# Attention heads in half legs: 256-query legs, a lead of 14 maxima, and score products issued in pairs of banks

## The reference

```python
x = L0_attn_x                                   # (2, 1024, 128)
h = _layernorm(x, axis=-1) * (1 + ca) + sa
q = (h @ Wq.T).reshape(N, S, 16, 8).transpose(0, 2, 1, 3)   # k and v likewise
energy = jnp.einsum('nhqd,nhkd->nhqk', q, k)
attn = jax.nn.softmax(energy / jnp.sqrt(jnp.float32(8)), axis=3)
out = jnp.einsum('nhql,nhld->nhqd', attn, v)
x = x + ga * out.transpose(0, 2, 1, 3).reshape(N, S, 128)
...
```

## Time and profile before

| what | value |
|---|---|
| median of 3 runs | 1158.91 us (1148.05 to 1160.96) |
| profiled execution, its own time | 1150.8 us |
| its span | 1149.3 us |
| PE busy | 1036.9 us, 90% |
| DVE busy | 968.1 us, 84% |
| ACT busy | 814.9 us, 71% |
| POOL busy | 520.9 us, 45% |
| attention with its score pass | about 61 to 381 us of the span |
| max products (L548) / scores (L667) / value products (L694) | 512 / 512 / 2048 instructions |
| reductions (L559) / exponentials (L675) | 256 / 512 |

### The profile page before, as it was taken

How to read it: one execution, slowest core, us unless ns; L and a number is a source line. 1 busy time by engine, 2 the same in 40 slices (tenths; PEclk the granted TensorE clock), 3 DMA queues, 4 the chain that set the end, 5 groups by cost and what they waited for, 6 DMA issues and landing times. The chain is left out here.

```text
span 1149.3 us, 21244 instructions
## 1 busy us (share of the span) xinstructions
PE 1036.9 (90%) x7771; PEld 648.5 (56%) x7771; DVE 968.1 (84%) x1309; ACT 814.9 (71%) x1621; POOL 520.9 (45%) x487
## 2 busy tenths in 40 slices
PE   6899999999999887889999999899999984699992
PEld 4222222222222334458998984468888964488992
DVE  6899999999995676979999996989999996767774
ACT  3279898999998644978888844888888922265561
POOL 5400431010101211027899991048999972256663
PEclk9779999999999988799999999899999995699996
DMA  5210100001000420107999980118999967311124
GB/s 158 69 43 15 30 16 21 25 16 30 15 2 2 130 56 2 58 2 178 244 248 224 223 205 3 58 43 193 234 242 224 242 144 253 41 43 41 43 48 121
DMA packets 58374, 114.40 MB, mean 100 GB/s; under 512 B 15406, under 2 KB 28718, under 8 KB 58272
## 3 DMA queue, kind: packets, MB, share of 16 engines
q0 software_dynamic: 14880, 50.23, 22.2%
q1 hardware_dynamic: 40152, 60.62, 16.8%
q10 hardware_dynamic: 3240, 2.20, 0.7%
HBM read 55.47 MB, written 9.13 MB: 56 GB/s over the span
## 5 line engine op out<-in xcount | busy, mean ns | idle before, releaser
L2245 PEld LDWEIGHTS m_pair<-filter_w,delta_x_t 128*128 128x128 f32 x2560 | 294.0, 192 | 43.1 <-issue 43.1
L559 DVE TENSOR_REDUCE neg_max<-max_ps 128x1 f32<-128x1024 f32 x256 | 295.6, 1214 | 15.2 <-PE max_ps L548 15.0
L2245 PE MATMUL m_pair<-filter_w,delta_x_t 128*128 128x112 f32 (+3 forms) x2560 | 298.5, 276 | 9.8 <-DVE h_t L2272 3.3
L675 ACT ACTIVATE exp_scores<-score_k 128x512 f32<-128x512 f32 x512 | 270.8, 605 | 28.4 <-PE score_k L667 22.7
L2221 ACT ACTIVATE decay<-delta,a_log 128x1024 f32<-128x1024 f32 x128 | 145.7, 1142 | 49.7 <-DVE normed L2272 29.7
L548 PE MATMUL max_ps<-k_rows,q_rows 48*128 48x512 bf16 x512 | 163.0, 400 | 12.4 <-DVE neg_max L559 10.7
L2213 ACT ACTIVATE filter_w<-filter,b_t 128x112 f32<-128x112 f32 (+1 forms) x576 | 167.4, 374 | 0.0
L667 PE MATMUL score_k<-q_rows,k_rows 51*128 51x512 bf16 x512 | 163.0, 389 | 2.4 <-ACT exp_scores L675 0.6
L694 PE MATMUL av_ps<-exp_scores,v_cols 128*32 128x256 f32 x2048 | 158.2, 394 | 0.0
L568 POOL CAST neg_max_parts<-neg_max 128x16 bf16<-128x16 f32 x16 | 3.2, 197 | 235.0 <-DVE neg_max L559 235.0
L694 PEld LDWEIGHTS av_ps<-exp_scores,v_cols 128*32 128x32 f32 x2048 | 44.2, 109 | 92.0 <-ACT exp_scores L675 52.8
(11 more groups left out here) (335 smaller groups left out, 1631.4 us busy)
## 6 DMA issues: line engine op xcount, KB each, us to landing
c_row<-c_rows SPq DMA_DIRECT2D x64, 512.0 KB, 6.0
x_inner<-normed POOLq DMA_DIRECT2D x16, 512.0 KB, 6.5
delta_x<-mod_memory POOLq DMA_DIRECT2D x15, 512.0 KB, 8.1
delta_x<-x_inner POOLq DMA_DIRECT2D x15, 512.0 KB, 8.3
x_inner<-h_t POOLq DMA_DIRECT2D x14, 512.0 KB, 5.7
mod_memory<-h_t POOLq DMA_DIRECT2D x14, 512.0 KB, 9.2
mod_memory<-normed POOLq DMA_DIRECT2D x12, 512.0 KB, 8.8
gate_up_all<-in_gate_up_w SPq DMA_DIRECT2D x8, 512.0 KB, 7.3
```

Of the source, the lines that this page charges most:

```text
L559: ve.tensor_reduce(nm[leg % 2][:, 4 * j + qt:4 * j + qt + 1], mps[:, bank:bank + 2, :].rearrange("p a q -> p (a q)"), AX_X, ALU.max, negat ...
L675: ac.activation(pt[a % 4][:, HEADS[r % 4], :], eps[:, bank, :], ACT.Exp, scale=SC).then_inc(*exped.up())
L2245: mm = pe.matmul(vps[blk][:, lo:hi], self.duT[b][:, c, blk * P:(blk + 1) * P], wf[g % 3][:, lo:hi], start=True, stop=True)
```

## The change

A leg of 512 queries is worked in two *turns* of 256 queries. Each turn has 8 max tiles, its own split, transpose, copy and 4 DMAs (half as many rows and queries in each), and 16 score banks. There are 32 turns in place of 16, issued at the end of places 0 and 2. The lead is 14 tiles instead of 22.

A score bank now holds two heads by 256 queries for one block of keys. Two banks are filled together by four products of 51 x 256 that alternate between the row halves (head 1, head 0, head 3, head 2), at the first s of each "msms"; the second s issues nothing. A pair waits for both of its banks. ACT still does 512 exponentials of 128 x 512, and `pe_av` is called as often as before. `po_ones(2, NS)` moves behind the split of turn 0, and the first `sp_load` of quad 1 waits for it.

```diff
-            nr = sb("neg_max_rest", [P, 4, 4])
-            ms = [sb(f"neg_max_parts{s}", [P, 4, 3, 4], BF16) for s in range(2)]
-            mt = [sb(f"neg_max_rows{s}", [48, P], BF16) for s in range(2)]
+            nr = sb("neg_max_rest", [P, 4, 2])
+            ms = [sb(f"neg_max_parts{s}", [P, 4, 3, 2], BF16) for s in range(2)]
+            mt = [sb(f"neg_max_rows{s}", [24, P], BF16) for s in range(2)]
...
-            NLEG, NU, AHEAD = BH // 2, 16, 22
+            NLEG, NU, AHEAD = BH // 2, 8, 14
+            NTURN, HQ = 2 * NLEG, CH // 2
...
-            def tile_of(leg, k):
-                return ((0, 2, 1, 3)[k // 4], k % 4) if leg == 0 else (k // 8 * 2 + k % 2, k % 8 // 2)
+            def tile_of(turn, k):
+                j, q = ((0, 2, 1, 3)[k // 2], k % 2) if turn == 0 else (k // 4 * 2 + k % 2, k % 4 // 2)
+                return j, turn % 2 * 2 + q
...
+            def sp_max_turn(turn):
+                leg, q0 = turn // 2, turn % 2 * HQ
+                sp.wait_ge(turn_read.sem, turn + 1)
                 for j in range(4):
                     s, row = head_rows(leg, j)
...
+                    sp.dma_start(qp[row + KR:row + KM, s, leg % 2, q0:q0 + HQ].rearrange("a (k q) -> a k q", k=2),
+                                 mt[turn % 2][6 * j:6 * j + 6, :]).then_inc(*max_in[turn % 2].up(16))
...
-            HEADS = (1, 3, 0, 2)
+            HEADS = ((1, 3), (0, 2))
+            def pe_score_pair(turn, r, banks):
+                leg, q0, kt = turn // 2, turn % 2 * HQ, r // 2
+                if r == 0:
+                    pe.wait_ge(max_in[turn % 2].sem, 64 * (turn // 2 + 1))
+                for _, free in banks:
+                    wait_from(pe, *free)
+                for c in range(2):
+                    for i, (bank, _) in enumerate(banks):
+                        s, row = head_rows(leg, HEADS[i][c])
+                        mm = pe.matmul(eps[:, bank, c * HQ:(c + 1) * HQ], kp[row:row + KM, s, kt * P:(kt + 1) * P],
+                                       qp[row:row + KM, s, leg % 2, q0:q0 + HQ], start=True, stop=True)
+                        if c:
+                            mm.then_inc(*score_mm.up())
...
             def score(e):
+                if e < 16 * NTURN and e % 2 == 0:
+                    banks = []
+                    for i in range(2):
+                        banks.append(score_bank())
+                        read.append((exped.sem, e + i + 1))
+                    pe_score_pair(e // 16, e % 16, banks)
+                    for i in range(2):
+                        ac_exp((e + i) // 16, (e + i) % 16, banks[i][0])
...
                     max_turn(0)
+                    po.wait_ge(*split.at())
+                    po_ones(2, NS)
+                    sp.wait_ge(*rows_set.at())
                     for half in range(2):
                         sp_load(1, half)
...
-                po.wait_ge(*part_lo.at())
-                po_ones(2, NS)
-                sp.wait_ge(*rows_set.at())
...
+                if place % 2 == 0 and n // 2 + 1 < NTURN:
+                    max_turn(n // 2 + 1)
                 if place == 2 and leg + 1 < NLEG:
-                    max_turn(leg + 1)
```

More of the change, by code:

```diff
@@ L544, in pe_max_score @@
                         pe.wait_ge(*first_half.at())
-                    elif k == (0 if leg else 8):
+                    elif k == (0 if turn else 4) and turn % 2 == 0:
                         pe.wait_ge(*loaded_at[leg // 2])
@@ L576, in max_score @@
             def max_score(v):
-                leg, k, half = v // 2 // NU, v // 2 % NU, v % 2
-                if leg >= NLEG:
+                turn, k, half = v // 2 // NU, v // 2 % NU, v % 2
+                if turn >= NTURN:
                     return
-                pe_max_score(leg, k, half)
+                pe_max_score(turn, k, half)
                 if half:
-                    ve_max_score(leg, k)
+                    ve_max_score(turn, k)
                     if k == NU - 1:
-                        po_max_parts(leg)
@@ L587, in pe_max_turn @@
-            def pe_max_turn(leg, bank, free):
-                pe.wait_ge(split.sem, 4 * leg + 4)
+                        po_max_parts(turn)
+            def pe_max_turn(turn, bank, free):
+                pe.wait_ge(split.sem, 4 * turn + 4)
                 wait_from(pe, *free)
                 pe.transpose(eps[:, bank, 0:64].bitcast(BF16)[0:3 * NU, :],
-                             ms[leg % 2][:].rearrange("p h a k -> p (h a k)"), self.identb[:]).then_inc(*max_turned.up())
-            def ac_max_turn(leg, bank):
-                ac.wait_ge(max_turned.sem, leg + 1)
-                wait_from(ac, max_in[leg % 2].sem, 64 * (leg // 2))
-                ac.activation(mt[leg % 2][:], eps[:, bank, 0:64].bitcast(BF16)[0:3 * NU, :], ACT.Copy).then_inc(
+                             ms[turn % 2][:].rearrange("p h a k -> p (h a k)"), self.identb[:]).then_inc(
+                                 *max_turned.up())
@@ L597, in ac_max_turn @@
+            def ac_max_turn(turn, bank):
+                ac.wait_ge(max_turned.sem, turn + 1)
+                wait_from(ac, max_in[turn % 2].sem, 64 * (turn // 2))
+                ac.activation(mt[turn % 2][:], eps[:, bank, 0:64].bitcast(BF16)[0:3 * NU, :], ACT.Copy).then_inc(
                     *turn_read.up())
-            def sp_max_turn(leg):
-                sp.wait_ge(turn_read.sem, leg + 1)
+            def sp_max_turn(turn):
+                leg, q0 = turn // 2, turn % 2 * HQ
+                sp.wait_ge(turn_read.sem, turn + 1)
@@ L631, in po_divide, with max_turn @@
                     rc[leg % 2][:][:, :, :, None].to_broadcast([P, 4, 4, HD]), ALU.mult).then_inc(*divided.up())
-            def max_turn(leg):
+            def max_turn(turn):
                 bank, free = score_bank()
-                pe_max_turn(leg, bank, free)
-                ac_max_turn(leg, bank)
-                sp_max_turn(leg)
+                pe_max_turn(turn, bank, free)
+                ac_max_turn(turn, bank)
+                sp_max_turn(turn)
                 read.append(turn_read.at())
```

66 lines of the change are left out of this document (28 added, 38 removed).

## The result

The change ran in 1341.32 us (median of six; 1310.28 to 1350.8), the kernel before beside it in 1155.82 (1144.7 to 1161.74). The ratio is 1.142, with a 95% interval of 1.1298 to 1.1542; it is taken from the faster executions of each kernel alone, and the two medians would give 1.16. The direction was forecast; the size was not: 1189 us was predicted, with 1209 as the upper end. The profiled execution took 1344.45 us, near the median. What it shows is in all eight executions on record (one took 1373.96 us): their granted clocks over the span are 0.80 to 0.85, where the profiled execution of the kernel before had 0.938.

A forecast was written before the change was run, and what follows sets the result against it. TensorE was taken to set the pace, gapless in 13 stretches a leg. Lead -9.4, legs +46.9 (+3.1 us over 15.1 legs) and ones and loads +0.5 gave +38 on 1150.8: 1189 us, range 1168 to 1209.

The forecast's parts named there:

- The clock: TensorE in the attention, 200 to 300 us of the kernel before: granted clock 1.00, the 2.4 GHz level.
- Score pairs: TensorE's stretches between max products: one row half gets 512 more columns, +0.213 us in 13 stretches, 2.77 us a leg.
- A: Rival: TensorE slips half-wide scores between max products at no cost, only turns are added; 1145 us, 6%.
- C: Rival: two more weight loads of 0.093 us are exposed in each stretch, +36 us; 1225 us, 8%.
- D: Rival: products of one half follow at a shorter spacing, 0.131 us a stretch; 1173 us, 5%.
- Is a pair held up by its banks?: Score banks awaiting exponentials: a loop of 1.0 to 1.1 us, under the new stretch of 1.32, so no hold-up.
- Lead: Before the first score: 14 max tiles instead of 22, 8 x 1.18 us, so -9.4 us.
- E: Rival: turn 0 comes late behind POOL or DMAs, so the lead is not won; 1198 us, 6%.
- Long stretch: The stretch of three max tiles from place 0 to place 1 stays with DVE's three reductions, 3.37 us: 0 added.
- F: Rival: the long stretch falls to TensorE's own 2.24 us, 1.13 less a leg; 1172 us, 8%.
- B, DVE paces: Rival: alternation frees hidden slack in TensorE and a leg shrinks to DVE's 18.5 us; 1127 us, 6%.
- Tail: Scores alone after the last maximum, now 14 tiles: ACT's pace of 1.1 us a pair holds, 0; DVE's finishing 0 to 1 us.

The follow-up runs named there:

- run without the waits for GpSimd: The change with score products repeated early, max products repeated behind turns, GpSimd's gate rows cut and moved, VectorE's gate columns spread: 1228.32 us, ratio 1.0585.
- second max product issued twice: The kernel before, with the closing max product of each tile issued twice and no pairs: 1195.83 us, ratio 1.0338.
- even order: The change with one of its four order strings evened out, so that the stretch behind the turn has a value call: 1317.01 us.
- single scores: The change without pairs, each bank holding both heads of one row half, plus gate rows in two parts and an evened order string: 1153.06 us, ratio 0.999.
- repeated score products: The change with two half-wide score products of the other row half issued again beside each closing max product: 1243.23 us, ratio 1.0772.

## Why the prediction was wrong, step by step

- *The clock*, the step that failed. "At a granted clock of 1.00, the 2.4 GHz level" was read off the kernel before and carried to the changed one for every leg; no term, bound or rival let it move. The changed kernel lost some 140 us there: 1344.45 less 1204, an estimate of its time at 2.4 GHz (next point). The run without the waits for GpSimd shows it by taking it away: with products in place of waits and no late GpSimd, the same pairs and half legs run at 0.939.
- *Sum at 2.4 GHz*: 1189. The change's own order takes 23.30 us a leg there, 0.57 less than with the repeated max products (23.87). So the run without late GpSimd, 1223.31, less 15 x 0.57 = 9 for these and 10 for its slower stretch after the attention, gives 1204; some 5 us of that are its two dips. Forecast was a leg of 22.6; the 0.7 more, 15 times, is 11 of the 15 us between. This 1204 lies in the stated range, but no run measured it. (The upper end of the range, by its own terms, adds up to 1212 and not 1209, which changes nothing here.)
- *Score pairs*, +0.213 us in 13 stretches: right. The stretch is 1.32 us, and the second max product issued twice, which has only this in it, adds 2.77 us a leg. Rivals A, C and D fall with it. The 131 ns spacing of the Trainium skill (TensorE: Matmul & The Clock Gate, Back-to-back issue gap) is not what these products show; 0.213 us it is at 2.4 GHz.
- *"Is a pair held up by its banks? It is covered by the value call."* Right in the stretches, wrong behind the turns. There a bank is taken by the turned product, and where the next stretch has no value call the cover is gone: 0.68 + 0.60 us a leg in the place of the 0.1 that I took ("no row shows a wait of that kind. Bounds 0 and 0.5"). Both fall in the long stretch and partly take the place of its wait for VectorE. It runs from the first row to the second:

```profile
492.21 0.39 PE L550 MATMUL max_ps<-k_rows,q_rows 48*128 48x512 bf16 x1
...
496.49 0.39 PE L550 MATMUL max_ps<-k_rows,q_rows 48*128 48x512 bf16 x1
```

That is 4.28 us, against 3.37 + 0.24 + 0.1 = 3.71 in the forecast: 0.57 more. The turn without such waits costs 0.45 us instead of 0.24 (0.15 to the next max product at 482.20, and 1.62 instead of 1.32 for the stretch behind it). Together this is the 0.7 us by which a leg of 23.30 us is over the forecast, some 11 us in all. What the waits cost beyond is the clock, for which the sum had no term.
- *Lead*: the first score came at 51.26 us, 10.1 earlier (9.4 forecast), answering. Right, and E falls. In the change it is buried.
- *Long stretch* at 0: F had it give way by 1.13 us a leg. It grew, as said, so F is wrong.
- *B, DVE paces*: even where the clock is 1.00 a leg takes 23.30 us, not 18.5, and DVE is busy 21.38 of 25 us (481 to 506). Wrong.
- *Tail* at 0: from the last maximum to the last reciprocal it takes 24.68 us (551.76 to 576.44), against 30.67 before with 8 score pairs more at 1.1 us each, which leaves 21.9. So 3 us were missed, part of them at 1.2 GHz. What follows the last reciprocal is 768 us against 770.

What was settled: the loss comes with the pairs, it is a loss of clock, each fall in the profiles of the change and of its variants lies at or just behind a wait of TensorE, and most of it goes when products stand in these waits or beside the lone ones. Two levels hold themselves with the same program: the even order held 0.50 for over 300 us and 1.00 for the rest of the max pass. What stays open: why pairs are so much more easily tipped than single scores, why some waits lower the clock and others alike do not, and what at 372 us in the even run raised it; no row distinguishes them. The runs with products in the waits both remove waits and add products, so they do not tell these two apart. Of the share of narrow products (32 us) and of half legs (79 us) only the medians speak.

Most falls in the change follow waits for banks of PSUM, and nearly all of these go when products fill them. The Trainium skill (TensorE: Matmul & The Clock Gate, A second HAM failure mode: psum-queue depth-cycling) tells of a kernel in which TensorE idles briefly between groups of products as it cycles through banks, and its clock goes up and down; the trace agrees, with idle times of 0.68 and 0.60 us. The trace also shows more than a level that goes up and down: at 130 to 140 us TensorE has 10.00 busy us of 10 and stays at 1.2 GHz.

## What to carry to other kernels

A granted clock of 1.00 in the profile of before belongs to that mix of products, not to the chip: a change that thins the products out, or puts even a short wait behind a step that recurs, gets a rival in which the clock falls, priced as the same stretch at 1.2 GHz (here 2.40 for 1.32 us). Look at what each bank is freed by at the places where the pattern breaks (turns, results, loads), not only in the regular stretch, and at what stands in GpSimd's queue ahead of a short step that TensorE waits for. And to find out whether a clock is lost, add work: repeated products alone made the change 98 us faster by the medians.

## What the runs showed of the hardware

- TensorE can be busy 100% of the time and stay at 1.2 GHz: 19.91 to 20.00 of 20 us in the windows of the even order from 80 to 360 us, at 0.50, until it rose at 372 us and stayed at 1.00 with the same products to 532 us.
- How fast the clock comes back depends on the mix: 4 to 8 us with single scores (0.65 at 138 to 142 us, 1.00 from 146), 4 to 11 with the repeated score products, 6 to 113 us in the change (down at 263, up at 269; down at 122, up at 235), and 322 from the first score in one run of the even order.
- Short waits can lower it, and their length does not decide. In the rows shown waits of 1.95 us and more did. With single scores 1.73 us did in one run at 136.82 and 1.72 us at 180.70 did not; 1.16 us in the kernel before did not. With pairs 0.68 with 0.60 behind it did in four of seven, a single one of 0.57 or 0.68 in one of nine, and a single 0.18 in three of eleven.
- A product issued twice in a half that is alone costs its column time and nothing else: 0.213 us for 512 columns, 2.77 us over a leg of 13.
